# Seventy instead of sixty-five sorted edge groups in a graph network kernel, and another split of h

## The reference, cut to what matters

```python
agg = segment_sum(x[src], dst) / max(cnt, 1)        # layer 1, the same with h in layer 2
h = relu(agg @ W_l + b_l + x @ W_r)
x = layernorm(x + (h2 @ W_out + b_out))
...
m = selu(concat(x[src], edge_attr) @ W1a + b1a) @ W1b + b1b
mean = segment_sum(m, dst) / max(cnt, 1)
x = layernorm(x + selu(concat(x, mean, u[0]) @ W2a + b2a) @ W2b + b2b)
```

## Time and profile before

| | us |
|---|---|
| median of 3 runs | 2545.67 (2545.4 to 2546.12) |
| the profiled execution | 2547.18 |
| its span, first to last instruction | 2545.4 |
| stage 1, to VectorE's last one-hot | 603 |
| stage 2, to the first gather | 543 |
| stage 3 | 1400 |

### The profile page before, as it was taken

How to read it: one execution, slowest core, us unless ns; L and a number is a source line. 1 busy time by engine, 2 the same in 40 slices (tenths; PEclk the granted TensorE clock), 3 DMA queues, 4 the chain that set the end, 5 groups by cost and what they waited for, 6 DMA issues and landing times. The chain is left out here.

```text
span 2545.4 us, 54296 instructions
## 1 busy us (share of the span) xinstructions
PE 2084.5 (82%) x19234; PEld 1539.5 (60%) x19234; DVE 1637.0 (64%) x3320; ACT 1015.8 (40%) x2319; POOL 1845.8 (73%) x1864
## 2 busy tenths in 40 slices
PE   1899999989989998984788888888878888867753
PEld 1555565555545555553676676777767777766753
DVE  6899999996455564554566666666666666643433
ACT  3787877874000000013344344444433444433322
POOL 5546768676777777777777777777777777777775
PEclk9999999999999999985899999998999999986665
DMA  8368786777769877824433333333333333332212
GB/s 298 111 231 224 228 264 180 250 198 134 210 208 253 237 210 232 241 59 109 123 74 74 71 80 74 77 76 72 76 77 74 80 74 74 72 71 51 51 41 46
DMA packets 524456, 342.56 MB, mean 135 GB/s; under 512 B 398996, under 2 KB 476495, under 8 KB 520781
## 3 DMA queue, kind: packets, MB, share of 16 engines
q1 hardware_dynamic: 407075, 267.01, 38.2%
q0 software_dynamic: 54240, 57.31, 10.3%
q10 hardware_dynamic: 62890, 14.87, 2.9%
HBM read 201.55 MB, written 137.36 MB: 133 GB/s over the span
## 5 line engine op out<-in xcount | busy, mean ns | idle before, releaser
L987 POOL DMA_INDIRECT A_sb<-source_terms,src_cur x1092 | 1049.1, 961 | 332.9 <-issue 327.4
L938 POOL DMA_INDIRECT sorted_edges<-pm_row,pm_to x520 | 575.4, 1107 | 183.6 <-issue 154.1
L1871 DVE TENSOR_TENSOR arena<-iota_code,arena 128x2048 f16<-128x2048 f16 (+1 forms) x392 | 435.5, 1179 | 19.6 <-PE cnt_ps L1416 17.3
L1082 ACT ACTIVATE A_sb<-cnt_ps 128x392 f32 (+1 forms) x784 | 383.8, 499 | 135.9 <-PE cnt_ps L1416 86.2
L1545 PE MATMUL agg_ps<-A_sb,arena 128*128 128x448 f16 x1911 | 378.6, 355 | 0.0
L1416 PEld LDWEIGHTS cnt_ps<-arena 128*128 128x128 f16 x3136 | 191.1, 100 | 225.7 <-issue 161.4
L1416 PE MATMUL cnt_ps<-arena 128*128 128x98 f16 x3136 | 280.3, 214 | 44.5 <-ACT A_sb L1082 27.1
L1545 PEld LDWEIGHTS agg_ps<-A_sb,arena 128*128 128x128 bf16 x1911 | 186.1, 99 | 165.0 <-issue 5.3
L1647 PE MATMUL agg_ps<-A_sb 128*65 128x48 f32 x2184 | 179.5, 243 | 123.1 <-DVE A_sb L2208 123.1
L1647 PEld LDWEIGHTS agg_ps<-A_sb 128*65 128x65 f32 x2184 | 165.7, 158 | 138.4 <-DVE A_sb L2208 130.4
L1423 PE MATMUL agg_ps<-A_sb,arena 128*65 128x448 f16 x686 | 243.3, 355 | 0.0
(11 more groups left out here) (308 smaller groups left out, 3505.7 us busy)
## 6 DMA issues: line engine op xcount, KB each, us to landing
counts_matrix<-A_sb SPq DMA_DIRECT2D x12, 5488.0 KB, 17.4
A_sb<-counts_matrix SPq DMA_DIRECT2D x12, 5488.0 KB, 18.7
arena<-in_edge_attr_dram SPq DMA_DIRECT2D x90, 256.0 KB
sorted_edges<-zrow SPq DMA_DIRECT2D x13, 1716.0 KB
arena<-sorted_edges SPq DMA_DIRECT2D x169, 128.0 KB
A_sb<-source_terms,src_cur POOLq DMA_INDIRECT x1092
overlapping_rows<-A_sb SPq DMA_DIRECT2D x1, 13056.0 KB, 39.4
pm_row<-in_edge_attr_dram ACTq DMA_DIRECT2D x46, 256.0 KB
```

The source lines that it names most:

```text
L938: pool.indirect_dma_start(out=sorted_d, out_offset=bass.IndirectOffsetOnAxis(ap=pm_to[:, k, j:j + 1], axis=0), in_=pm_row[:, k, j, :], in_ ...
L987: pool.indirect_dma_start(out=gath[k][:, j * F:(j + 1) * F], out_offset=None, in_=p_d, in_offset=bass.IndirectOffsetOnAxis(ap=src_cur[k][: ...
L1082: act.activation(Asb(half)[:, :, bass.ds((b * BG + k) * GROUP, GROUP)].rearrange("p b (w j) -> p b w j", j=PAIR), cnt_ps[k % 2][:, 0:SUB * ...
L1871: ins = dve.tensor_tensor(hot_rows[:, slots], iota_code[:, 0:n, :].unsqueeze(1).to_broadcast([P, AT_ONCE * SUB // 2, n, 2]), turned[:, bas ...
```

## The change

Five things. (1) NR goes from 13 to 14, so 70 groups are sorted and 132 are left for slots. (2) Blocks 4 to 13 of stage 1 sort two groups each, so 21 are sorted in stage 1 and 49 later, as before. (3) The split of h: a part is now the upper half of each fp32 value, read in place as bf16 with a step of two. VectorE makes the two remainders (`split_h` behind one-hot group 48 of a block, in blocks 2 to 13, and twice behind them); GpSimd only packs the three upper halves into `hpart`, the second and third as each remainder is made. The store waits for the third pack. (4) In layer 2 ScalarE's queue issues a block's group loads behind the move of h2, behind the root and behind the moves at the block's end; those ahead of the move of h2 and behind `move_agg2` (the next block's start) are gone. (5) The loop of gathers leaves its last round to the unrolled part. The tiles grow with NR from 676 to 728, the units from 169 to 182, and `LAST_STEP` goes from 111 to 106.

```diff
-NR = 13
+NR = 14
-TWO_IN = (4, 8, 11, 12, 13)
+TWO_IN = (4, 5, 6, 7, 8, 9, 10, 11, 12, 13)
+SPLIT_AT = 48
...
+        h_rest = [t.rearrange("p c f -> p (c f)") for t in (hs[:, :, :], hr, h1m[1])]
+        h_top = [t.bitcast(BF16).rearrange("p (n t) -> p n t", t=2)[:, :, 1] for t in h_rest]
+        h_out = [hpart[:, i].rearrange("p c f -> p (c f)") for i in range(3)]
...
             def store_h(m, half):
-                sp.wait_ge(h_split, m + 1)
+                sp.wait_ge(h_split, 3 * m + 3)
...
-                pool.tensor_copy(hpart[:, 0], hs[:, :, :]).then_inc(pool_dep, 1)
-                pool.wait_ge(pool_dep, m * 4 + 1)
-                pool.sem_inc(pool_at, 1)
-                pool.tensor_tensor(hr[:, :, :], hs[:, :, :], hpart[:, 0], ALU.subtract).then_inc(pool_dep, 1)
...
-                pool.tensor_copy(hpart[:, 2], hr[:, :, :]).then_inc(h_split, 1)
+                pool.tensor_copy(h_out[0], h_top[0]).then_inc(h_split, 1)
+                pool.wait_ge(rest_made, m * 2 + 1)
+                pool.tensor_copy(h_out[1], h_top[1]).then_inc(h_split, 1)
+                pool.wait_ge(rest_made, m * 2 + 2)
+                pool.tensor_copy(h_out[2], h_top[2]).then_inc(h_split, 1)
...
-            with pool.Fori(1, NEGC // DEEP) as r:
+            with pool.Fori(1, (NEGC - 1) // DEEP) as r:
...
-                if s is not None and (s == 1 or LAYER2[s - 1] == 4):
-                    load_group(FIRST[s] + 2)
                 act.wait_ge(h2_turned, m + 1)
                 act.activation(h2T, t2_ps[:, 0:SBN], ACT.Copy).then_inc(h2_moved, 1)
                 if s is not None:
-                    load_group(FIRST[s] + 3)
+                    load_group(FIRST[s] + LAYER2[s] - 1)
...
+                if s is not None:
+                    load_group(FIRST[s + 1])
...
                 if s is not None:
-                    load_group(FIRST[s] + 4)
+                    load_group(FIRST[s + 1] + 1)
+                    if s + 1 < NSB and LAYER2[s + 1] == 4:
+                        load_group(FIRST[s + 1] + 2)
                     move_agg2(s)
-                    load_group(FIRST[s] + 5)
...
+                if s >= 2:
+                    make_hot(s, half, begun, SPLIT_AT)
+                    begun = SPLIT_AT
+                    split_h(s - 2)
...
+            def split_h(m):
+                dve.wait_ge(h_relu, m + 1)
+                if m > 0:
+                    dve.wait_ge(h_split, 3 * m)
+                dve.tensor_tensor(h_rest[1], h_rest[0], h_top[0], ALU.subtract).then_inc(rest_made, 1)
+                dve.wait_ge(rest_made, m * 2 + 1)
+                dve.tensor_tensor(h_rest[2], h_rest[1], h_top[1], ALU.subtract).then_inc(rest_made, 1)
...
             for q in range(IN_STAGE1, IN_STAGE1 + 3):
                 slot_group(q)
                 sort_group(q + 1)
+                if q == IN_STAGE1:
+                    split_h(NSB - 2)
...
+            split_h(NSB - 1)
             slot_group(IN_STAGE1 + 3)
```

More of the change, by code:

```diff
@@ L441, in build @@
         sp_at = pool_at = act_at = pe_at = dve_at = sem("waited")
-        pool_dep, idx_made, zm_made = sem("pool_dep"), sem("idx_made"), sem("zm_made")
+        rest_made, idx_made, zm_made = sem("rest_made"), sem("idx_made"), sem("zm_made")
         part_in, parts_in = [sem(f"part_in{i}") for i in range(3)], sem("parts_in")
@@ L496, in build @@
         lanes_hot, LANES_HOT = win_dve, 2 * SETS * NSB
-        unit_z, UNIT_Z = h_split, NSB
-        unit_selu, UNIT_SELU = pool_dep, 4 * NSB
+        unit_z, UNIT_Z = h_split, 3 * NSB
+        unit_selu, UNIT_SELU = rest_made, 2 * NSB
         unit_msg, UNIT_MSG = agg_ready, NSB
@@ L887, in split_h @@
                 pool.sem_inc(pool_at, 1)
-                pool.tensor_copy(hpart[:, 0], hs[:, :, :]).then_inc(pool_dep, 1)
-                pool.wait_ge(pool_dep, m * 4 + 1)
-                pool.sem_inc(pool_at, 1)
-                pool.tensor_tensor(hr[:, :, :], hs[:, :, :], hpart[:, 0], ALU.subtract).then_inc(pool_dep, 1)
-                pool.wait_ge(pool_dep, m * 4 + 2)
-                pool.sem_inc(pool_at, 1)
-                pool.tensor_copy(hpart[:, 1], hr[:, :, :]).then_inc(pool_dep, 1)
-                pool.wait_ge(pool_dep, m * 4 + 3)
-                pool.sem_inc(pool_at, 1)
-                pool.tensor_tensor(hr[:, :, :], hr[:, :, :], hpart[:, 1], ALU.subtract).then_inc(pool_dep, 1)
-                pool.wait_ge(pool_dep, m * 4 + 4)
-                pool.sem_inc(pool_at, 1)
-                pool.tensor_copy(hpart[:, 2], hr[:, :, :]).then_inc(h_split, 1)
+                pool.tensor_copy(h_out[0], h_top[0]).then_inc(h_split, 1)
[3 more added lines that the diff above has]
+                pool.tensor_copy(h_out[2], h_top[2]).then_inc(h_split, 1)
             gather_fine(0, FEW)
@@ L1003, in _ @@
                 gather(k, k)
-            with pool.Fori(1, NEGC // DEEP) as r:
+            with pool.Fori(1, (NEGC - 1) // DEEP) as r:
                 for k in range(DEEP):
                     gather_next(r * DEEP + k, k)
-            for g in range(NEGC // DEEP * DEEP, NEGC):
+            for g in range((NEGC - 1) // DEEP * DEEP, NEGC):
                 gather_next(g, g % DEEP, edges_of(g))
```

## The result

The changed kernel takes 2627.08 us (median of 4 runs, 2622.81 to 2630.43) where the kernel before took 2545.89 beside it: a ratio of 1.0314, 95% interval 1.0298 to 1.0329. That is slower, as forecast, but by 81 us, not by 10, and outside the range. The profiled execution has a span of 2621.1 us (2545.4 before) at the same mean granted clock, 0.917.

The account below looks back on a forecast made before the run. Bounds taken: VectorE in stage 1, GpSimd's scatters in stage 2, on average its gathers in stage 3. Terms of +11.6, +8.7 and -10.2 us sum to +10.1: 2555.8 us on the median, range 2540 to 2570.

Parts of the forecast that it names:

- the groups: Stage 1, five blocks get a second group: blocks 4 to 11 +13.6 us, loads and packs costing no wait.
- T: End of VectorE's one-hot work in stage 1, 603 us before; forecast to move by +11.6, ends +3 and +18.
- Rival C: Stage 1: packs hold VectorE for their whole length, some 1.1 us a block more; 2567 us, chance 0.13.
- The other terms of stage 1: Lighter split saves 3.1 us a block, VectorE's subtractions add 1.45, packs 0.8: two-group block 41.35, with clock dips 42.0.
- The turn: Stage 1 to 2: three blanks, not two, start at T + 6.5 and release GpSimd's scatters at T + 41.
- Rival A: Turn and stage 1: blanks drain fast (release T + 33.3), packs cost VectorE nothing; 2544 us, no change, chance 0.22.
- Stage 2: GpSimd's scatters set its end: 510.5 us from release to first gather, at T + 551.5; +8.7 us.
- Rival B: TensorE's chain ends stage 2, so late loads save 25 us of stalls; total -8.6, 2537 us, chance 0.15.
- The T + 533 for TensorE's own path: Stage 2: TensorE's own path ends at about T + 533, ahead of GpSimd's T + 551.5.
- Stage 3: Unit chain takes over as bound: 1059.6 us bare, 1070.4 with clock dips, -4.7; with closing slots -10.2 us together.
- the closing slots: Stage 3's end: GpSimd is one gather and more ahead behind the units, so first closing slots are short, -5.5 us.
- The direction: Whole kernel: slower, chance 0.63 (main forecast 0.50 plus Rival C); same 0.22, faster 0.15.

Follow-up runs that it names:

- run 1: Changed kernel with SyncE loading the next block's groups before it stores h: 2594.34 us, 1.0193 of the kernel before.
- run 2: Changed kernel with VectorE's split of h at group 44, ahead of the second group's slots, not at 48: 2569.63 us, 1.0093 of before.
- run 9: The kernel of run 2 with GpSimd waiting for the one-hots of group 50 before the second pack: 2585.49 us, 1.0119 of before.
- run 12: Kernel before with only ScalarE's late group loads of layer 2 added: 2555.53 us beside 2553.01, 1.0013.
- run 7: The kernel of run 2 with 65 groups, nine two-group blocks, three groups in every layer 2 block: 2544.70 us, 1.0003 of before.
- run 13: 65 groups and the old five two-group blocks of the kernel before, the whole new split (subtractions and three copies) on VectorE: 2533.56 us, 0.9961.
- run 3: Changed kernel with the three packs moved from GpSimd to VectorE, behind its subtractions: 2579.99 us, 1.0138 of before.
- run 5: Changed kernel with the old split (GpSimd's two subtractions and three casts), keeping 70 groups and late loads: 2586.78 us, 1.0156 of before.
- run 10: Changed kernel with VectorE waiting for the end of its second subtraction before the next one-hot: 2583.70 us beside 2553.01, 1.0125.
- its second kernel: The kernel of run 13 with the nine two-group blocks of run 7, three groups in every layer 2 block: 2524.67 us beside 2553.01, 0.9903.
- run 11: Changed kernel with plain fp32 h as operand of VectorE's second subtraction, on a low-clock chip: 3753.80 us, 1.0469 of before.
- run 4: Changed kernel with GpSimd casting whole fp32 values in place of packing upper halves: 2627.64 us, 1.0334 of before.
- run 8: Changed kernel with GpSimd memsets ahead of the second pack: three, 3824.97 us, 1.0501 (low clock); nine, 2632.38 us, 1.0345.

## Why the prediction was wrong, step by step

**The step that failed** is in *the groups*: "the loads land 5 to 7 us into the next block and its first sort comes at 10.5. I cost that at nothing; were the packs 5 us later, VectorE would wait there." They were some 12 us later. The chain of queues was named rightly, down to the place where VectorE would wait; what I missed is the pack behind it. I let each pack wait for one VectorE instruction at most, as the casts of the earlier trace rows did, and the last end 3.2 us ahead of T. The second took 13.26 us. T came to +60.1 in place of +11.6, 48.5 us more; VectorE's waits for end points, put at nothing, add up to 52.3. They are not the whole mechanism: with the loads out of the way (run 1) only 27 us came back, since the held operation also filled GpSimd's queue; without the hold (run 2) all 48 did.

Rival C had the right two engines and the wrong loser: it let the packs hold VectorE. VectorE lost nothing: its twelve one-hots beside the held pack take 12.20 us, six in 6.1, as beside scatters. Its cost went through GpSimd's queue and SyncE's, not through VectorE's time.

The Trainium skill, SBUF — State Buffer, "Who interferes with whom", has the two wait for one another's whole instruction. Block 5 of run 9 agrees: the pack waited for the rest of one one-hot. The held pack does not: it waited for thirteen instructions on end, 13.26 us, and there the measurement decides.

**The other terms of stage 1 were right.** The block that I put at 42.0 (41.35 without a dip of the clock) takes 47.1 with 6.2 us of that wait: 40.9. With the pack let in (run 2) T is 615.2, forecast 614.6. That they agree to 0.6 us is partly luck, as T alone moved by 7 us between executions of the same code (run 12).

**The turn** was right. Three blanks are issued at 671.6 = T + 8.5 (forecast T + 6.5), and GpSimd's wait is the one named:

```profile
704.16 0.98 POOL L934 DMA_INDIRECT sorted_edges<-pm_row,pm_to  x1 [17.38 <-DMA sorted_edges<-zrow]
```

Release at T + 41.1, forecast T + 41; the wait before it was 17.4 us, forecast some 19. The blanks went out 2 us later than forecast and took 2 us less. Rival A, with T + 33, falls.

**Stage 2**: first gather at 1216.7 = T + 553.6, forecast T + 551.5. From the release to the first gather it took 512.6 us, forecast 510.5; GpSimd's scatters waited 1.2 us for VectorE's slots there, 6.3 before. In the eight other kernels with the same 49 groups at the usual clock the first gather came at T + 547.1 to T + 562.2, so 2 us of agreement is closer than the forecast could be. Rival B would have needed TensorE's chain to set the end; run 12 shows no gain in the kernel's time from the late loads. The T + 533 for TensorE's own path had no row, and was too late: with 45 groups the first gather came at T + 517 and T + 521 (runs 7 and 13).

**Stage 3, the second wrong term**: forecast -10.2, measured +4.8. The mechanism was right: the chain of the unit steps takes over. The z additions' wait for gathers fell from 72.8 us in 27 to

```profile
  DMA A_sb<-source_terms,src_cur: 14.8, 2
```

and slots stand 11.51 and 5.49 apart. The sizes were off. The 102 unit slots took 1080.8 us, 21.2 above the bare chain of 1059.6, where I allowed 10.8. I had argued that most dips of the granted clock came behind a wait for gathers and would go with it; they did not: the record of the clock has 22 stretches at half speed in the unit slots, 24 before. And the closing slots took 249.3 (250.2 before), not 5.5 less: `gather_next` lets a gather go only once an earlier slot is through, which would leave little lead to spend; only the first closing slot was short, 8.98 us where before had 10.59. At the usual clock, in one execution each, nine kernels with 132 slots took 1402.6 to 1411.9 us for stage 3, five with 137 (before among them) 1389.4 to 1401.9: five groups more in the table lengthen stage 3 by some 10 us and don't shorten it.

**The direction** was right, with 0.63, but not for the price that I named. Without a held pack 70 groups are 0.9 to 1.6% slower than before (runs 2, 3, 5 and 10): stage 1 and the turn cost about what the forecast says, and stage 3 brings a loss and not the gain. With the groups of before, the new split all on VectorE gains 0.4% (run 13); the 1.0% of its second kernel, and the nothing of run 7, come with another distribution of the groups too.

**Still open**: why one-hots that follow on the second subtraction without a pause keep GpSimd out. Its operand, the pack's operand and the moment of the start are excluded by runs 11, 4 and 8; a pause behind it is enough to end it. It needn't be a subtraction, nor fp32: behind VectorE's third copy, bf16 to bf16, it is the same (runs 3 and 13), and behind a scan of the sort it is not. What the two have in common that the scan lacks wasn't tried.

## What to carry to other kernels

When an operation of GpSimd goes next to a run of VectorE instructions without a pause, cost it by both ends, one instruction and the whole run, look for the hold in all of GpSimd's operations and not only in those that you moved, and follow what stands behind it in GpSimd's queue and in every queue that waits for it. Put it where VectorE's operations wait for one another, or make VectorE wait once, 0.04 us, behind the operation that feeds it. If neither is possible, let the held one be an operation that nobody waits for. And when a stage's bound is about to change hands, cost the new bound with all the disturbances that it had under the old one.

## What the runs showed of the hardware that I had not expected

- A GpSimd operation of 0.6 us can be kept out for 13.26 us by VectorE instructions, each 1.0 to 1.2 us, that follow on one another: with nine memsets (run 8) in all eleven blocks where the pack was asked for behind the second subtraction, and in none of the nine in run 9 where the one-hots had begun behind a pause.
- Not only copies are kept out. The issue of an indirect DMA by GpSimd, 0.9 to 2.1 us otherwise, took 12.52 us (window gather, run 1) and 12.16 us (scatter, run 13) in the same place.
- It goes the other way too: at the end of block 7 of the changed kernel the first two packs ran back to back (380.7 to 381.9) and VectorE's second subtraction took 1.90 us in place of 0.69.
- A pause of 0.04 us behind the subtraction is enough for GpSimd to get in (run 10).
- A pack, 112x512 with a stride of two, takes VectorE 0.42 us and GpSimd 0.61.
- Two chips granted TensorE 0.77 to 0.79 of its clock over the whole kernel, and the kernel before took 3638 and 3592 us in place of 2546, while the one-hots and gathers took as long as elsewhere (run 7).
